# Second attention of a four-layer model: scores in three fp32r passes of split q and k, and a second context batch prepared beside the expert blocks

## What is computed

```python
x = x + _L0_xattn_ref(ctx_1024, _layernorm(x), ...)      # latents attend to the context, 16 heads of 64
x = x + _L0_ffn_ref(_layernorm(x), ...)                  # a shared FFN plus top-1 of 16 experts
x = x + _L1_xattn_ref(_layernorm(x), ctx_1024, ctx_1024, Wq, bq, Wk, bk, Wv, bv, Wo, bo)
x = x + _L1_ffn_ref(_layernorm(x), ...)                  # 8 experts, each chooses its tokens

def _L1_xattn_ref(query, key, value, ...):               # 8 batches, 256 queries, 256 keys, 16 heads of 16
    q = query @ Wq.T + bq; k = key @ Wk.T + bk; v = value @ Wv.T + bv
    scores = jnp.einsum('bhqd,bhkd->bhqk', q, k) * scale
    probs = jax.nn.softmax(scores, axis=-1)
    out = jnp.einsum('bhqk,bhkd->bhqd', probs, v)
    return out.transpose(0, 2, 1, 3).reshape(B, S, EMB) @ Wo.T + bo
```

## Time and profile before

| | |
|---|---|
| runs | 1604.76, 1611.44, 1614.6 us |
| profiled execution | 1609.12 us |
| its span | 1607.4 us |
| PE, DVE, ACT, POOL busy over the span | 91%, 59%, 54%, 41% |
| first attention | up to 699 us |
| mixture | 699 to 996.5 us |
| of it the expert blocks | 785 to 968 us |
| second attention | 996.5 to 1247 us |
| last layer, with its norm and gate | from 1247 us |

### The profile page before, as it was taken

One profiled execution on the slowest core, in us unless ns is written; L12 is line 12 of the kernel. 1 busy time (PEld: TensorE's weight loads), 2 busy tenths in 40 slices (PEclk: granted clock), 3 DMA queues, 4 the chain that ended last, 5 costly groups with the idle time before them and its releaser, 6 DMA issues. The chain is left out here.

```text
span 1607.4 us, 28452 instructions
## 1 busy us (share of the span) xinstructions
PE 1457.6 (91%) x9884; PEld 1192.5 (74%) x9884; DVE 942.7 (59%) x1745; ACT 870.0 (54%) x2176; POOL 665.3 (41%) x978
## 2 busy tenths in 40 slices
PE   4999999999999999969799998999998549999995
PEld 3888887878787878758788896565664438888885
DVE  5776767676767676746311115777777644444442
ACT  3886877777877787724211114665654224444442
POOL 6514444444343431232300004654421026777774
PEclk9999999999999999979899998899999569999998
DMA  4400000000000000011599972100000413454442
GB/s 133 172 1 21 1 21 2 21 3 2 21 2 21 2 1 1 2 40 49 196 313 316 316 277 46 21 14 21 8 2 1 154 50 106 127 122 118 121 122 27
DMA packets 74447, 120.26 MB, mean 75 GB/s; under 512 B 7008, under 2 KB 55136, under 8 KB 74304
## 3 DMA queue, kind: packets, MB, share of 16 engines
q1 hardware_dynamic: 63600, 101.76, 19.4%
q0 software_dynamic: 10704, 16.65, 5.1%
HBM read 99.78 MB, written 18.61 MB: 74 GB/s over the span
## 5 line engine op out<-in xcount | busy, mean ns | idle before, releaser
L508 ACT ACTIVATE a_p<-a_s,a_negmax 128x512 f32<-128x512 f32 x256 | 176.2, 688 | 110.9 <-DVE a_negmax L632 61.1
L632 DVE TENSOR_REDUCE a_negmax<-a_s 128x1 f32<-128x512 f32 x256 | 176.3, 689 | 74.3 <-PE a_s L371 67.9
L273 POOL TENSOR_TENSOR a_o_l<-a_o,a_o_h 128x256 fp32r<-128x256 f32 x64 | 46.9, 735 | 297.2 <-ACT a_o_h L533 297.2
L1660 ACT ACTIVATE h_probs<-h_scores,h_negmax 128x256 f32<-128x256 f32 x256 | 118.0, 473 | 87.5 <-DVE h_negmax L1843 87.0
L380 PEld LDWEIGHTS a_t<-ident,a_p 128*128 128x128 f32 x1024 | 122.3, 140 | 51.3 <-issue 22.8
L380 PE MATMUL a_t<-ident,a_p 128*128 128x128 f32 x1024 | 156.7, 276 | 0.6 <-DVE a_pT L647 0.6
L2110 POOL TENSOR_TENSOR n_w_l<-n_raw,n_w_h 128x768 fp32r<-128x768 f32 x64 | 118.1, 1846 | 74.5 <-ACT n_w_h L2153 74.5
L398 PE MATMUL a_out_p<-a_pT,a_v 128*64 128x256 f32 x1024 | 124.6, 385 | 0.0
L370 PE MATMUL a_s<-a_k_hl,a_q_hh 128*128 128x512 f32 x256 | 106.2, 415 | 2.3 <-issue 1.6
L1843 DVE TENSOR_REDUCE h_negmax<-h_scores 128x4 f32<-128x1024 f32 x64 | 78.0, 1219 | 47.2 <-PE h_scores L1768 46.4
L1779 PEld LDWEIGHTS h_turned<-ident,h_probs 128*128 128x128 f32 x512 | 56.6, 145 | 65.5 <-issue 49.5
(11 more groups left out here) (420 smaller groups left out, 4400.3 us busy)
## 6 DMA issues: line engine op xcount, KB each, us to landing
e_w_in<-in_L_ffn_gate_up_proj SPq DMA_DIRECT2D x31, 1024.0 KB, 6.9
n_raw<-in_L_ffn_w SPq DMA_DIRECT2D x64, 384.0 KB, 3.0
e_w_out<-in_L_ffn_down_proj SPq DMA_DIRECT2D x31, 512.0 KB, 5.4
rows_in<-a_zeros SPq DMA_DIRECT2D x1, 3968.0 KB, 15.6
e_rows<-rows_in SPq DMA_DIRECT2D x31, 128.0 KB, 5.2
rows_out<-e_result POOLq DMA_DIRECT2D x31, 128.0 KB, 4.7
a_both<-in_ctx SPq DMA_DIRECT2D x8, 256.0 KB, 2.7
a_both<-in_x SPq DMA_DIRECT2D x8, 256.0 KB, 3.0
```

The lines of the kernel that those rows point to most:

```text
L508: act.activation(probs[j][:, :], scores[j % 2][:, :], ACT.Exp, bias=negmax[:, j:j + 1], accum_out=total[:, r % 2, j % 2, j // 2:j // 2 + 1 ...
L632: dve.tensor_reduce(negmax[:, j:j + 1], scores[j % 2][:, :], AX.X, ALU.max, negate=True).then_inc(max_set, 1)
L1660: ins = act.activation(probs[s % 4][:, j, :], scores[s % 2][:, j // 2, j % 2, :], ACT.Exp, bias=negmax[:, s % 4, j:j + 1], accum_out=total ...
```

## The change

1. `score` takes three passes instead of one: q_h·kz_h, q_l·kz_h, q_h·kz_l, all fp32r, each for both row groups, six matmuls a step, summed in PSUM.
2. ACT makes kz_h of the next batch (`high_k`, two instructions of 128x512) after step 2, and q_h (`high_q`, one) after step 6. DVE makes kz_l (`low_k`, two instructions) in step 6. POOL makes q_l (`low_q`, one), behind `low_o(b, 0)`. `spread_k` leaves POOL. The first score of a batch now waits for `ql_set` and `kzl_set`.
3. On ACT, high_x moves from step 5 to step 4 and high_ctx from 4 to 5. k_full and q_full have one buffer each, so set_q waits for the last ql_set.
4. The context of batch 0 is loaded after the weights of block 2 (it was loaded before all of them), and that of batch 1 after the weights of block 4. They are split at blocks 1 and 6. At the start of the second attention nothing of context 1 is loaded or split any more.
5. For batch 0 the mixture now makes kz_h (ACT), kz_l (DVE, ahead of unit 12), q_h (ACT) and q_l (DVE, after normalise(1)).
6. Tiles move into the space of the spare weights (ctx_raw, k_full, q_full, v0, e_result), with waits on `wl_set` before their first use.

The core of the diff:

```diff
@@ mixture, SP @@
+                def load_context(b):
+                    wait(sp, ctxl_set, b)
+                    sp.dma_start(g.ctx_raw, ...[:, :, b * S:(b + 1) * S]).then_inc(ctx_in, 16)
...
-                sp.dma_start(g.ctx_raw[:, :, :], ...[:, :, 0:S]).then_inc(ctx_in, 16)
...
                 load_weights(2)
+                sp.wait_ge(wl_set, 4)
+                load_context(0)
                 for j in range(AHEAD, BLOCKS):
                     load_rows(j)
                     load_weights(j)
+                    if j == AHEAD + 1:
+                        load_context(1)
@@ mixture, POOL @@
-                pool.wait_ge(ctxh_set, 1)
-                pool.tensor_tensor(g.ctx_l0[:, :, :], g.ctx_raw[:, :, :], g.ctx_h0[:, :, :], ALU.subtract).then_inc(ctxl_set, 1)
                 for j in range(BLOCKS):
                     pool.wait_ge(result_set, j + 1)
                     pool.dma_start(results_dram[:, j, :], result[j % 2][:, :]).then_inc(stored[j % 2], 16)
+                    if j in SPLIT_AT:
+                        b = SPLIT_AT.index(j)
+                        pool.wait_ge(ctxh_set, b + 1)
+                        pool.tensor_tensor(g.ctx_l[b][:, :, :], g.ctx_raw, g.ctx_h[b][:, :, :], ALU.subtract).then_inc(ctxl_set, 1)
@@ mixture, ACT: kz and q of batch 0 @@
-                for m in range(KC):
-                    for e in range(2):
-                        ins = act.activation(g.kz0[:, m, e, :], g.k_full[:, m, :], ACT.Copy, scale=g.mask[:, e:e + 1])
-                ins.then_inc(kz_set, 1)
+                for e in range(2):
+                    ins = act.activation(g.kz_h0[:, :, e, :], g.k_full, ACT.Copy, scale=g.mask[:, e:e + 1])
+                ins.then_inc(kzh_set, 1)
...
+                act.wait_ge(q_set, 1)
+                act.activation(g.q_h0[:, :, :], g.q_full, ACT.Copy).then_inc(qh_set, 1)
@@ mixture, DVE, after the blocks @@
+                dve.wait_ge(kzh_set, 1)
+                for e in range(2):
+                    ins = dve.scalar_tensor_tensor(g.kz_l0[:, :, e, :], g.k_full, g.mask[:, e:e + 1], g.kz_h0[:, :, e, :],
+                                                   ALU.mult, ALU.subtract)
+                ins.then_inc(kzl_set, 1)
...
                 normalise(1)
+                dve.wait_ge(qh_set, 1)
+                dve.tensor_tensor(g.q_l0[:, :, :], g.q_full, g.q_h0[:, :, :], ALU.subtract).then_inc(ql_set, 1)
@@ second attention, POOL @@
-                low_ctx(1)
                 normalise(FIRST)
...
-                    if b + 1 < NB:
-                        spread_k(b + 1)
...
                     low_o(b, 0)
+                    if b + 1 < NB:
+                        low_q(b + 1)
                     if b + GATHERED + 1 < NB:
                         gather(b + GATHERED + 1)
@@ second attention, ACT @@
+                def high_k(b):
+                    act.wait_ge(k_set, b)
+                    wait(act, scored, STEPS * (b - 1))
+                    for e in range(2):
+                        ins = act.activation(kz_h[b % 2][:, :, e, :], k_full, ACT.Copy, scale=mask[:, e:e + 1])
+                    ins.then_inc(kzh_set, 1)
+                def high_q(b):
+                    act.wait_ge(q_set, b)
+                    act.activation(q_h[b % 2][:, :, :], q_full, ACT.Copy).then_inc(qh_set, 1)
...
+                        if s == 2 and b + 1 < NB:
+                            high_k(b + 1)
-                        if s == 5 and b + FIRST < NB:
+                        if s == 4 and b + FIRST < NB:
                             high_x(b + FIRST)
+                        if s == 6 and b + 1 < NB:
+                            high_q(b + 1)
-                        if s == 4 and b + 2 < NB:
+                        if s == 5 and b + 2 < NB:
                             high_ctx(b + 2)
@@ second attention, PE @@
                     if s == 0:
-                        wait(pe, q_set, b)
-                        wait(pe, kz_set, b)
+                        wait(pe, ql_set, b)
+                        wait(pe, kzl_set, b)
                     wait(pe, exp_set, n - 1)
-                    for j in range(2):
-                        ...
-                        ins = pe.matmul(scores[s % 2][:, j, :, :], q[b % 2][rows, m, half * P:(half + 1) * P],
-                                        kz[b % 2][rows, m, :, :], start=True, stop=True)
+                    passes = ((q_h, kz_h), (q_l, kz_h), (q_h, kz_l))
+                    for i, (q, kz) in enumerate(passes):
+                        for j in range(2):
+                            ...
+                            ins = pe.matmul(scores[s % 2][:, j, :, :], q[b % 2][rows, m, half * P:(half + 1) * P],
+                                            kz[b % 2][rows, m, :, :], start=(i == 0), stop=(i == len(passes) - 1))
@@ second attention, DVE @@
+                        if s == 6 and b + 1 < NB:
+                            low_k(b + 1)
```

More of the change, by code:

```diff
@@ L836, in run_mixture @@
         e_silu, e_hidden = ([w[:, :].rearrange("p (c t) -> p c t", t=P) for w in units] for units in (silu, hidden))
-        result = [sb(f"e_result{i}", [P, D]) for i in range(2)]
+        result = [g.spare[1][:, 4 * S + i * D:4 * S + (i + 1) * D] for i in range(2)]
         stats, mv = sb("g_stats", [P, 2, 6]), sb("g_mv", [P, 2, 2])
@@ L1546, in _, with low_q @@
             def _(sp):
-                for b in range(1, NB):
-                    wait(sp, ctxl_set, b - 1)
-                    sp.dma_start(ctx_raw[:, :, :], ctx_dram[:, :, b * S:(b + 1) * S]).then_inc(ctx_in, 16)
+                for b in range(2, NB):
+                    wait(sp, ctxl_set, b - 2)
+                    sp.dma_start(ctx_raw, ctx_dram[:, :, b * S:(b + 1) * S]).then_inc(ctx_in, 16)
             @block.gpsimd
             def _(pool):
-                def spread_k(b):
-                    pool.wait_ge(k_set, b)
-                    for m in range(KC):
-                        for e in range(2):
-                            ins = pool.tensor_scalar(kz[b % 2][:, m, e, :], k_full[:, m, :], mask[:, e:e + 1], None, ALU.mult)
-                    ins.then_inc(kz_set, 1)
+                def low_q(b):
+                    pool.wait_ge(qh_set, b)
+                    pool.tensor_tensor(q_l[b % 2][:, :, :], q_full, q_h[b % 2][:, :, :], ALU.subtract).then_inc(ql_set, 1)
                 def low_ctx(b):
-                    pool.wait_ge(ctxh_set, b)
-                    pool.tensor_tensor(ctx_l[b % 2][:, :, :], ctx_raw[:, :, :], ctx_h[b % 2][:, :, :],
+                    pool.wait_ge(ctxh_set, b - 1)
+                    pool.tensor_tensor(ctx_l[b % 2][:, :, :], ctx_raw, ctx_h[b % 2][:, :, :],
                                        ALU.subtract).then_inc(ctxl_set, 1)
@@ L1645, in set_k @@
                     act.wait_ge(k_done, b)
-                    wait(act, kz_set, b - 1)
+                    wait(act, kzl_set, b - 1)
                     for m in range(KC):
@@ L1889, in measure, with low_k @@
                         ins.then_inc(x_measured, 1)
+                def low_k(b):
+                    dve.wait_ge(kzh_set, b)
+                    for e in range(2):
+                        ins = dve.scalar_tensor_tensor(kz_l[b % 2][:, :, e, :], k_full, mask[:, e:e + 1], kz_h[b % 2][:, :, e, :],
+                                                       ALU.mult, ALU.subtract)
+                    ins.then_inc(kzl_set, 1)
                 def low_x(b):
@@ L2361, in program @@
             g.bias_v, g.bias_o = keep(ctx, "bias_v", [P, g.D]), keep(ctx, "bias_o", [P, g.D])
-            g.ctx_raw = keep(ctx, "ctx_raw", [P, g.KC, g.S])
-            g.ctx_h0, g.ctx_l0 = (keep(ctx, f"ctx_{part}0", [P, g.KC, g.S], F32R) for part in "hl")
-            g.q0, g.k_full, g.kz0 = keep(ctx, "q0", [P, g.KC, g.S]), keep(ctx, "k_full", [P, g.KC, g.S]), keep(ctx, "kz0", [P, g.KC, 2, g.S])
-            g.v0, g.mask = keep(ctx, "v0", [P, 2, 16, 32]), keep(ctx, "mask", [P, 2])
+            g.ctx_raw, g.k_full, g.q_full = (g.spare[0][:, i * g.KC * g.S:(i + 1) * g.KC * g.S].rearrange("p (c t) -> p c t", c=g.KC)
+                                             for i in range(3))
+            g.v0 = g.spare[1][:, 0:2 * 16 * 32].rearrange("p (c h e) -> p c h e", c=2, h=16)
+            g.ctx_h, g.ctx_l = ([keep(ctx, f"ctx_{part}{i}", [P, g.KC, g.S], F32R) for i in range(2)] for part in "hl")
+            g.q_h0, g.q_l0 = (keep(ctx, f"q_{part}0", [P, g.KC, g.S], F32R) for part in "hl")
+            g.kz_h0, g.kz_l0 = (keep(ctx, f"kz_{part}0", [P, g.KC, 2, g.S], F32R) for part in "hl")
+            g.mask = keep(ctx, "mask", [P, 2])
             with ExitStack() as inner:
```

48 lines of the change are left out of this document (27 added, 21 removed).

## The result

After the change the median is 1634.89 us (1632.66 to 1639.57, 4 runs) against 1612.72 us (1604.76 to 1614.6, 4 runs) of the kernel before, a ratio of 1.0156 with an interval of 1.0131 to 1.018. The profiled execution took 1634.69 us.

| stage | before, us | after, us |
|---|---|---|
| up to the mixture's first matmul | 701.34 | 703.27 |
| mixture, from there to the first score | 295.23 | 295.14 |
| second attention, first score to the load of the last layer's gate | 251.15 | 274.5 |
| from there to the end | 359.68 | 360.07 |

The account below looks back on a forecast made before the run. PE was taken to lead the second attention, DVE close; expert blocks near PE and DMA limits. Batch 0 -4, batches 1 to 6 +3, last batch +1.3, mixture +1, clock +25: +26 on 1609.1, 1635 us, range 1600 to 1670.

Parts of the forecast that it names:

- late q_l: At batch ends, score 0 waits for POOL's low_q until about +5.7 us; the maximum of step 0 comes 2.9 us later.
- slow clock: Behind seven batch ends, PE's 4.8 us idle brings 1.2 GHz; 3.6 us each, +25 us in all.
- Score: Each attention score on PE: three passes with row groups side by side take 0.87 us, a gain of 0.19.
- second rival: In the score, passes don't run side by side or wait for loads: 1.23 to 1.56 us, some 1660 us; chance 0.14.
- Second part of a batch: Steps 3 to 7: faster scores 0.95, DVE's xT_h wait 1.20, copies found ready 0.3; together 2.4 us saved.
- What was costed at nothing: Added ACT and DVE work is hidden; low_k fits DVE's 2.91 us idle before the last maximum, leaving 1.5 us.
- Batch 0: First batch of the second attention: no delay, -2.4 us, and its start gains 1.22 and 0.4 us: -4.
- Mixture: Context 1's load among the expert blocks delays block 5's rows; bounds 0 and 2.5 us, taken +1.
- batches 1 to 6: Middle batches go from 29.8 to 30.3 us without the clock: six times 0.5, +3 us.
- last batch: The last batch has the 2.9 us delay but no projections making PE late, -1.6: +1.3 us.
- the clock stays: Rival at the batch ends: the clock stays at 2.4 GHz despite the gap; 1610 us, chance 0.22.
- q_l isn't late: Rival at the batch ends: score 0 doesn't find q_l late, delay and slow clock gone; -20, 1589 us, chance 0.10.

Follow-up runs that it names:

- e1: The changed kernel with POOL making q_l of the next batch before low_o(b, 0) instead of behind it; 1595.61 us, ratio 0.993.
- e2: The changed kernel with 16 extra fp32r matmuls, result unread, ahead of the wait for q_l at batch starts after batch 0; 1616.42 us, ratio 1.0046.
- e3: The kernel before plus an unread POOL subtraction behind low_o(b, 0), for which score 0 of the next batch waits; 1664.94 us, ratio 1.0354.
- e4: The kernel before with only ACT's high_x moved to step 4 and high_ctx to step 5; 1603.6 us, ratio 0.9967.
- e5: The kernel of e1 with ACT's high_x back in step 5 and high_ctx back in step 4; 1602.12 us, ratio 0.9951.
- e6: The kernel of e1 with context 1 loaded and split at the start of the second attention, as before the change; 1594.5 us, ratio 0.9921.
- e7: The kernel of e1 with POOL's batch 0 reordered: batch 3's normalisation before the first inverse, low_q(1) before low_o(0, 0); 1594.27 us, ratio 0.9923.
- e8: The kernel of e1 with a score's six matmuls reordered: all three passes of one row group, then of the other; 1596.57 us, ratio 0.9915.

## Why the prediction was right

It forecast 1635.0 us (1600 to 1670) by a late q_l and a slow clock. Both were there, and each was shown by an experiment of its own: e1 takes the wait away and both losses go, e2 leaves the wait and takes the clock's share alone, e3 brings both into the old kernel.

- **Score.** 0.87 forecast, 0.89 measured. The three pairs start 0.34 and 0.23 us apart, so neither do the row groups queue nor do the passes wait for their weights, and the second rival falls. The rule of the Trainium skill that was set against it (TensorE: Matmul & The Clock Gate, Part 3, "The mechanism": weight loads overlap running matmuls only where the row group differs) would have given a longer score; the trace doesn't agree with it here. The same section names a background weight buffer as a second case in which loads run ahead, and the trace fits that one.
- **Late q_l.** From the maximum of step 7 at 1089.78, score 0 came at +5.56 (forecast +5.7). Its maximum came at +6.60 in e2 (forecast +6.7), that is 2.8 us late (forecast 2.9). The chain of the prediction (exponentials, high_o, low_o, low_q) is the one that the trace shows.
- **Second part of a batch.** This step was mis-sized: 1.8 us saved where 2.4 were forecast. Two terms were too large. The wait for xT_h was taken at its full 1.20 us; behind it DVE now waits for the next score, 0.40 us in e4 and 0.23 in after, so 0.8 to 1.0 was left (e4, e5). The 0.3 us for copies found ready didn't show. Also the exchange saves nothing in batches 6 and 7, which have no high_x; the forecast counted it in batch 6. Without the clock a batch in the middle is 30.8, not 30.3 us.
- **What was costed at nothing.** low_k was to take 1.4 us of DVE's idle before the last maximum and leave 1.5. It took 1.41 (e1's row at the end of this text) and 1.40 are left in after.
- **Clock.** 3.6 us a batch end forecast, 3.3 measured (34.18 - 30.84). The span of half speed was bounded by 5 and 11 us of work, taken as 8.2, and the rows of after show 7.9. That it came so close is luck. Both bounds were counted from the middle of a slow stretch: by the granted clock of before, half speed lasted from 777.1 to 790.6 and from 992.2 to 1012.7. From the first matmul behind the idle (779.53 and 993.25) that is 11.1 and 19.5 us of time. The same working with these would have given 5.0 to 9.2 us a batch end, 35 to 65 us in all. What the rows could show was that the clock would fall, not for how long.
- **Batch 0.** From its first maximum to that of step 7 it went from 28.40 to 20.74 us, 7.7 less, where 4 were forecast. e6 against e1 gives 2.3 of it to the context that is there early. The rest comes with the faster score, the exchange (1.3 in e4's batch 0) and the clock, which came back after 10.2 us instead of 20.5; they were not measured apart. The prediction took the first batch's clock as given. e6 shows that the wait for the context isn't what held it; what does is not known, only that all kernels with fp32 scores had 20.5 and all with three passes 10.2.
- **Mixture.** +1 forecast, 0 in the two profiles: the stretch of the blocks (first gate matmul to last up matmul) took 0.8 us longer, 0.2 more went behind them, and 1.0 was gained ahead of block 0. The forecast looked for the delay at block 5, whose rows were issued 2.1 us later (805.70, against 803.56 in the earlier trace rows). PE's waits for the rows of blocks 5 and 6, after:

```profile
808.83 0.44 PE L1079 MATMUL m_small<-ident,e_rows 128*128 128x128 f32 x2 [0.65 <-DMA e_rows<-rows_in]
...
816.65 0.44 PE L1079 MATMUL m_small<-ident,e_rows 128*128 128x128 f32 x2 [2.07 <-DMA e_rows<-rows_in]
```

For block 5 PE waited no longer than before (0.65, against the 0.83 of the earlier trace rows). The wait came at block 6, 2.07 us, where before there was none. Over all profiled executions the blocks were 1.4 us longer with context 1 among them (e6).
- **End of the layer.** The forecast had no term for what stands behind the last score. It took 2.7 us less, up to the last projection: the same turn, behind the same idle, ran at half clock before and at full clock after.

```profile
1234.81 1.94 PE L1779 MATMUL h_turned<-ident,h_probs 128*128 128x128 f32 x8 [0.41 <-DVE h_probsT L1853]
```

```profile
1262.71 1.16 PE L1823 MATMUL h_turned<-ident,h_probs 128*128 128x128 f32 x8 [0.41 <-DVE h_probsT L1897]
```

Why the clock fell there in one kernel and not in the other stays open.
- **Sum.** The attention lost 23.4 us of the 25.3 forecast for it. Part by part, with e2 against before for what isn't the clock and after against e2 for the clock:

| part | forecast, us | measured, us |
|---|---|---|
| batch 0 | -4 | -7.2 |
| batches 1 to 6 | +3 | +7.0 |
| last batch | +1.3 | +2.3 |
| clock, seven batch ends | +25 | +24.1 |
| behind the last score | nothing | -2.7 |

The mechanism and its largest term are right. But the parts without the clock missed by 1 to 4 us each, some too hopeful and some too gloomy, and offset one another. That the total came within 0.1 us of the forecast is luck, beyond the luck in the clock's length.

Of the rivals, that the clock stays (1610) didn't happen, though e2 comes near to what it would have been: 1616.42. That q_l isn't late (1589) is what e1 built: 1595.61.

**The better version.** e1, e6, e7 and e8 all lie at 1594 to 1597 us and can't be told apart; each beats the kernel before by 0.7 to 0.9% and, by the ratios to it, the one after by 2.2 to 2.4%. e1 is the simplest: the change as made, with low_q ahead of low_o.

## What to carry to other kernels

When a change adds an operand that an engine makes just in time, look at what stands ahead of it in that engine's queue, not at its duration: 1.26 us of subtraction cost 6.2 us a batch (34.2 - 28.0, half of it by the clock) since it stood behind an instruction that waits for the batch's last exponentials. Price an idle of TensorE twice, by the delay and by the half clock behind it, which here cost more than the delay. And when a wait is removed, count only the distance to the wait that comes next.

## What the runs showed of the hardware

**DVE and POOL take turns.** kz_l on DVE reads two tiles in SBUF. In e1 its two instructions take 1.41 us, and in e5, where POOL's split of the context falls beside them, 2.87. First e1, then e5's DVE (the first of the two by itself, then both), then e5's POOL:

```profile
1104.56 1.41 DVE L1938 SCALAR_TENSOR_TENSOR kz_l<-spare,mask,kz_h 128x512 fp32r<-128x512 f32 x2
```

```profile
1109.74 1.19 DVE L1938 SCALAR_TENSOR_TENSOR kz_l<-spare,mask,kz_h 128x512 fp32r<-128x512 f32 x1
1109.74 2.87 DVE L1938 SCALAR_TENSOR_TENSOR kz_l<-spare,mask,kz_h 128x512 fp32r<-128x512 f32 x2
```

```profile
1109.34 1.04 POOL L1630 TENSOR_TENSOR xn<-xn,h_p_rstd 128x512 f32<-128x512 f32 x1
1110.34 1.73 POOL L1587 TENSOR_TENSOR ctx_l<-spare,ctx_h 128x512 fp32r<-128x512 f32 x1
1112.03 1.71 POOL L1583 TENSOR_TENSOR q_l<-spare,q_h 128x512 fp32r<-128x512 f32 x1
```

The subtractions on POOL take 1.73 and 1.71 us instead of 1.27. Their ends alternate: POOL's xn 1110.38, the first kz_l 1110.93, ctx_l 1112.07, the second kz_l 1112.61, q_l 1113.74. Each of the last four ends some 0.55 us (DVE) or 1.13 us (POOL) after the one before it, a little under its length alone (0.70 and 1.27). So such a pair doesn't share, it takes turns. The Trainium skill says as much (SBUF — State Buffer, "Who interferes with whom": a DVE instruction with two SBUF inputs contends with a GpSimd one that reads SBUF), and the trace agrees. In e5 it fell into DVE's idle before the last maximum and cost no time that can be seen: the distance from step 6 to 7 is 5.73 us in e5 and 5.74 in e1.

**Row groups overlap out of program order.** In e8 the fourth matmul of a score (the first of the second row group) starts with the first, 0.34 us ahead of the second pair, which holds the program's second matmul. The Trainium skill (TensorE: Matmul & The Clock Gate, Part 3, "The mechanism") has matmuls start strictly in order; the records and the 0.90 us of that score speak against it for different row groups.

**The length of an idle didn't settle whether the clock falls.** Behind 4.6 us it fell each time. Behind 0.9 us in e5 it fell in batches 2, 3 and 7 and not in 1, 4, 5 and 6, and behind 0.41 us at the end of the layer in before and not in after.

**Half clock is not one price.** The same 4.6 us of idle was followed by 7.9 us of half-speed work with three-pass scores and by some 10.4 us with fp32 scores (e3), and cost 3.3 and about 5 us a batch. The 5 is an estimate: e3's 7.8 us a batch less the 2.8 of the wait, which e2 measured on the other kernel.
